# Adding B x u to one of the two states on TensorE, in PSUM, in 378 of 512 pairs of time steps

## Chip, cores and metric

One core of a Trainium2 chip. The metric is the device time of one execution of the kernel, in microseconds (us).

## What is computed

Two sequences of 1024 tokens with 512 channels go through a selective state-space layer (with a residual and a layer norm) and a gated feed-forward layer (with a residual and a layer norm), all in fp32. The core of it is the recurrence over time, with a state of 512 x 128 numbers for each sequence:

```python
def step(h, inp):
    dt, bt, ct, xt = inp
    h = jnp.exp(dt[:, :, None] * A) * h + (dt * xt)[:, :, None] * bt[:, None, :]
    y = jnp.einsum('bdn,bn->bd', h, ct)
    return (h, y)
...
x = _layernorm(x + (ys + x * D_param) @ out_proj_w.T)
x = _layernorm(x + (silu(x @ w_gate.T) * (x @ w_up.T)) @ w_down.T)
```

Here `dt`, `bt`, `ct` come from projections of a normalized and gated x, `u = dt * xt`, and B and C below are `bt` and `ct`.

## The kernel before

The state h has its index n (128) on the partitions and the 512 channels of a sequence in the free dimension. For each of the 1024 steps t and each of the two sequences b there are two VectorE instructions of 128 x 512: a product `a * h(t-1)` into PSUM (`m_ps`, line 708; one bank per sequence), and a sum into the ring `h` of seven steps (H_RING). The sum is a multiply-add `u * B + product` with B as a scalar for each partition (line 731), or, where another engine has multiplied u by B beforehand, a plain add (line 728). GpSimd does that for some even steps (line 615), ScalarE for others (line 1023).

The other engines supply and drain this loop:

- GpSimd spreads dt over diagonals (`dexp`, line 603), TensorE multiplies them by A (`exponents`, line 1223, four 32-row groups side by side) and ScalarE takes exp of the result into the ring `a` (line 1004). Each such round serves half the channels of four steps, so there is one for each pair of steps. The PSUM banks `p_ps` hold one round, so TensorE and ScalarE take turns on them.
- SP loads u of each step, broadcast to all partitions, from a scratch in DRAM into the ring `u_bc` of seven steps (line 472).
- TensorE computes y of a step from h and C (`y_row`, line 1299; 32-column matmuls, four side by side for two steps). It issues the y rows of steps t-2 and t-1 at each even t. ScalarE takes a window of 64 steps out at a time.
- Everything else (the projections for the chunk of 128 steps ahead, the output projection, layer norms and feed-forward for the chunk behind) is cut into pieces. `timetable` writes down in which half step ("slot") each piece stands, from gaps that are given by hand for each stage. All engines walk the same plan: two slots for each step, hence four for a pair. TensorE's pieces (`gu`, `down`, `sel`, `xp`, ...) share one PSUM bank, `work`, which ScalarE empties. A product piece (`product`, line 1059, or line 1199 for `down`) is four fp32 matmuls of 256 columns; the trace shows two records for each fp32 matmul.

All engines run their instructions strictly in the order in which they were written, with semaphores between them: `s_m` counts products, `s_h` sums, `s_y` y rows, `s_exp` the exponentials.

## Time and profile before

| | |
|---|---|
| median of 3 runs | 2670.15 us (2664.76 to 2670.43) |
| span of the profiled execution | 2662.4 us |
| VectorE busy | 2577.2 us, 97% of the span |
| TensorE busy (matmuls) | 2323.3 us, 87% |
| TensorE weight loads | 1281.6 us, 48% |
| ScalarE busy | 1836.4 us, 69% |
| GpSimd busy | 1030.8 us, 39% |

The span is the time from the first to the last instruction in one profiled execution; for that execution no other time is given. Busy times are unions of the records of an engine. In the names of the trace DVE is VectorE, ACT ScalarE, POOL GpSimd, PE TensorE's matmuls and PEld its weight loads.

### The profile page before, as it was taken

To read this page: it belongs to the slowest core of one execution; us is meant where nothing else is said; L and a number is where in the kernel's file an instruction comes from. 1 tells how busy PE (TensorE), PEld (TensorE's weight loads), DVE (VectorE), ACT (ScalarE), POOL (GpSimd) and SP (SyncE) were. 2 spreads that over 40 slices of the span, in tenths; PEclk is the share of its full clock that TensorE was granted. 3 is DMA by queue.
4 is the path that set the end of the run, shared out by engine and by line. 5 is a ranking of instruction groups with operands and counts; after the bars stand their busy time and mean duration, and the time that the engine had idled before them with its cause. 6 is when DMAs were issued, how large, how long until landed. Compare 5 with 4: busy or idle time off the path is not lost.

```text
span 2662.4 us, 48762 instructions
## 1 busy us (share of the span) xinstructions
PE 2323.3 (87%) x17036; PEld 1281.6 (48%) x17036; DVE 2577.2 (97%) x4160; ACT 1836.4 (69%) x2432; POOL 1030.8 (39%) x1031
## 2 busy tenths in 40 slices
PE   7867678999789987899889998899978998998898
PEld 4322234545345544555445553454534554465557
DVE  6999999999999999999999999999999999999892
ACT  5778767678676776667766777767867678653743
POOL 2343333443344433444334433344334443343320
PEclk8999999999899998999999999999989999999999
DMA  5666666777667776777767787677766777787784
GB/s 189 216 215 223 225 237 238 276 257 275 239 243 272 269 270 228 252 268 276 264 231 264 258 287 246 233 278 257 271 245 231 272 265 268 264 289 281 246 323 156
DMA packets 192064, 672.20 MB, mean 252 GB/s; under 512 B 20944, under 2 KB 26064, under 8 KB 191824
## 3 DMA queue, kind: packets, MB, share of 16 engines
q1 hardware_dynamic: 152432, 544.02, 57.8%
q10 hardware_dynamic: 39392, 125.06, 13.8%
q8 instruction: 140, 2.29, 0.3%
q14 instruction: 100, 0.82, 0.1%
HBM read 660.61 MB, written 8.39 MB: 251 GB/s over the span
## 4 chain that ended last, share of the span: by engine, by line
PE 45%; DVE 25%; ACT 14%; issue 11%; DMA 4%; DVEq 0%; ACTq 0%; POOL 0%; POOLq 0%
PE banks L1059 14%; PE banks L1223 11%; DVE h L731 11%; PE banks L1299 9%; DVE banks L708 9%; PE banks L1199 8%; ACT a L1004 6%; DVE h L728 5%; DMA U<-in_xT 2%; ACT L742 1%; ACT u_bc L1023 1%; DMA u_bc<-u_scratch 1%; PE banks L1151 1%; PE banks L1147 1%; DMA w_ring<-in_down_w 1%
## 5 line engine op out<-in xcount | busy, mean ns | idle before, releaser
L708 DVE TENSOR_TENSOR banks<-a,h 128x512 f32<-128x512 f32 x2048 | 1331.5, 692 | 6.9 <-ACT a L1004 6.9
L1004 ACT ACTIVATE a<-banks 128x2048 f32<-128x2048 f32 x512 | 960.3, 1876 | 510.1 <-PE banks L1223 464.8
L731 DVE SCALAR_TENSOR_TENSOR h<-u_bc,BCt,banks 128x512 f32<-128x512 f32 x1285 | 899.0, 734 | 5.9 <-PE banks L1299 5.8
L603 POOL TENSOR_TENSOR dexp<-spread,dt 128x512 f32<-128x512 f32 x512 | 538.5, 1052 | 815.2 <-DVE banks L708 765.7
L1299 PE MATMUL banks<-h,cz 128*32 128x512 f32 x4096 | 696.7, 618 | 97.6 <-DVE h L728 50.0
L1223 PE MATMUL banks<-dexp,A 32*128 32x256 f32 x8192 | 612.1, 414 | 149.6 <-ACT a L1004 147.8
L1223 PEld LDWEIGHTS banks<-dexp,A 32*128 32x128 f32 x8192 | 383.9, 191 | 474.7 <-ACT a L1004 354.5
L728 DVE TENSOR_TENSOR h<-u_bc,banks 128x512 f32<-128x512 f32 x763 | 489.8, 674 | 3.3 <-POOL u_bc L615 3.3
L1059 PE MATMUL banks<-vT,w_ring 128*128 128x256 f32 x1792 | 453.2, 396 | 18.7 <-ACT up L971 17.6
L1059 PEld LDWEIGHTS banks<-vT,w_ring 128*128 128x128 f32 x1792 | 326.0, 192 | 187.7 <-issue 108.8
L1023 ACT ACTIVATE u_bc<-u_bc,BCt 128x512 f32<-128x512 f32 x497 | 333.2, 713 | 61.7 <-DMA u_bc<-u_scratch 60.9
L615 POOL TENSOR_SCALAR u_bc<-u_bc,BCt 128x512 f32<-128x512 f32 x266 | 184.0, 692 | 379.7 <-DVE banks L708 379.7
L1299 PEld LDWEIGHTS banks<-h,cz 128*32 128x32 f32 x4096 | 109.0, 109 | 382.5 <-issue 370.0
L1199 PE MATMUL banks<-gated,w_ring 128*128 128x256 f32 x896 | 225.1, 394 | 16.0 <-ACT vT L976 8.9
L1199 PEld LDWEIGHTS banks<-gated,w_ring 128*128 128x128 f32 x896 | 162.1, 191 | 100.1 <-issue 65.4
L969 ACT ACTIVATE sg<-banks 128x256 f32<-128x256 f32 (+1 forms) x144 | 51.8, 360 | 143.4 <-PE banks L1059 141.9
L543 POOL TENSOR_TENSOR gated<-gated,sg 128x512 f32<-128x512 f32 x56 | 75.0, 1340 | 96.1 <-DVE banks L708 75.5
L546 POOL TENSOR_TENSOR gated<-gated,up 128x512 f32<-128x512 f32 x56 | 72.5, 1294 | 78.3 <-DVE banks L708 78.3
L742 ACT ACT_TABLE_LOAD x55 | 70.6, 1283 | 14.5 <-issue 12.3
L1059 PE MATMUL banks<-U,w_sel 128*128 128x256 f32 x256 | 70.5, 425 | 8.3 <-ACT dt L770 7.1
L973 ACT ACTIVATE sg<-sg,half 128x256 f32<-128x256 f32 (+1 forms) x144 | 71.4, 496 | 0.0
L1059 PEld LDWEIGHTS banks<-U,w_sel 128*128 128x128 f32 x256 | 51.2, 210 | 34.6 <-issue 15.7
(179 smaller groups left out, 1276.1 us busy)
## 6 DMA issues: line engine op xcount, KB each, us to landing
u_bc<-u_scratch SPq DMA_DIRECT2D x1021, 512.0 KB, 4.6
w_ring<-in_gu_w ACTq DMA_DIRECT2D x112, 512.0 KB, 5.0
w_ring<-in_down_w ACTq DMA_DIRECT2D x56, 512.0 KB, 5.3
a<-in_gu_w ACTq DMA_DIRECT2D x16, 512.0 KB, 5.6
a<-in_down_w ACTq DMA_DIRECT2D x8, 512.0 KB, 4.6
x_tok<-in_x_rows SPq DMA_DIRECT2D x15, 256.0 KB, 4.8
out_rows<-v ACTq DMA_DIRECT2D x15, 256.0 KB, 4.2
U<-in_xT ACTq DMA_DIRECT2D x7, 512.0 KB, 7.0
```

The source lines that it names most:

```text
L603: e.tensor_tensor(dexp[:, q % E_RING, :, :, :], spread[:, :].unsqueeze(1).unsqueeze(1).to_broadcast(shape), by_step[:, :, first:first + BS ...
L615: e.tensor_scalar(part, part, BCt[c % 2][:, 0, tl:tl + 1], 1.0, ALU.mult, ALU.mult).then_inc(s_zp, 1)
L708: e.tensor_tensor(m_ps[:, b, :], a[:, blk % A_RING, b, s, :], h[:, (t - 1) % H_RING, b * D:(b + 1) * D], ALU.mult).then_inc(s_m, 1)
L728: e.tensor_tensor(h[:, t % H_RING, part], u_bc[:, t % U_RING, part], m_ps[:, b, :], ALU.add).then_inc(s_h, 1)
L731: e.scalar_tensor_tensor(h[:, t % H_RING, part], u_bc[:, t % U_RING, part], BCt[c % 2][:, 0, b * TB + tl:b * TB + tl + 1], m_ps[:, b, :], ...
L742: e.preload_act_table_set("natural_log_exp_and_others")
L1004: e.activation(dst.rearrange("p b t (x j) -> p x (b t) j", j=GP), src.rearrange("p g (i r j) -> p (g i) r j", i=PAIR, j=GP), ACT.Exp, scal ...
L1023: e.activation(part, part, ACT.Copy, scale=BCt[c % 2][:, 0, b * TB + tl:b * TB + tl + 1]).then_inc(s_za, 1)
L1059: last = e.matmul(dst, w, x, start=i == 0, stop=i == len(pairs) - 1)
L1199: last = e.matmul(dst, tile[:, sub * (HB // 4) + i, :], hidden(x, hb), start=hb == 0, stop=hb == HB - 1)
L1223: last = e.matmul(dst[:, g, i * COLS:(i + 1) * COLS], A[rows, q % 2 * PAIR + i, :], lays, start=True, stop=True)
L1299: last = e.matmul(y_ps[group * GP:(group + 1) * GP, :], cz[:, first:first + GP], h[:, t % H_RING, b * D:(b + 1) * D], start=i == 0, stop=i ...
```

## The change

Steps are now walked in pairs (t, t+1), t even. From step 128 on, a pair is marked (`on_x`) where the summed load figures of ScalarE's pieces (`LOAD`) stay within a budget of 20 for each pair, with what exceeds it carried over to the next. 378 of 448 pairs are marked, 54 in each chunk. In a marked pair:

- VectorE leaves out the sum of (t, 1). TensorE adds it instead: a matmul with one row, B of the step as weights (1 x 128) and u as the moving operand (1 x 512), accumulates onto the product in PSUM (`add_inputs`).
- The product of (t+1, 1) reads h of (t, 1) there, in PSUM, and is written to `m_sb` in SBUF. It waits for the matmul (`s_acc`).
- ScalarE copies h of (t, 1) from PSUM to the ring `h` for y (`state`), after that product; the product of (t+2, 1), which overwrites the bank, waits for the copy (`s_hx`).
- The product of (t+1, 0) stands directly behind the sum of (t, 0).

For this, u comes in two rings (`u_bc` of seven steps for b = 0, `v_bc` of four for b = 1, which skips marked steps), and rows of u and B together (640 numbers) are written to a second DRAM scratch once for each chunk and loaded one by one into `x_row` by SP. B of sequence 1 is transposed for that by one more matmul per chunk. ScalarE's scaling of u is kept only in the first chunk and for b = 0, GpSimd's only for steps that are not marked. GpSimd's work in marked pairs waits for another product than before. In the last two chunks' feed-forward work the gap before `down` is 4 slots instead of 0.

```diff
+        on_x, busy = {}, 0
+        for t in range(FIRST_X, SEQ, 2):
+            busy = max(0, busy + sum(LOAD.get(stage, 0) for stage, _ in at_steps(t, 2)) - X_BUDGET)
+            if not busy:
+                on_x[t] = len(on_x)
...
+                e.dma_start(u_bc[:, slot, :], u_scratch[t, 0, :].partition_broadcast(P)).then_inc(d_u[slot], 16)
+                if t not in on_x:
...
+                    e.dma_start(v_bc[:, k % V1_RING, :], u_scratch[t, 1, :].partition_broadcast(P)
+                                ).then_inc(d_v[k % V1_RING], 16)
+                if t + X_AHEAD in on_x:
...
+                    e.dma_start(row_of(k), x_scratch[t + X_AHEAD:t + X_AHEAD + 1, :]).then_inc(d_row[k % X_RING], 16)
...
+            def product(t, b, dst):
+                blk, s = t // BS, t % BS
+                src = h[:, (t - 1) % H_RING, b * D:(b + 1) * D]
+                if b and t - 1 in on_x:
+                    e.wait_ge(s_acc, on_x[t - 1] + 1)
+                    src = m_ps[:, b, :]
+                elif t:
+                    e.wait_ge(s_h, sum_of(t - 1, b))
+                if b and t - 2 in on_x:
+                    e.wait_ge(s_hx, on_x[t - 2] + 1)
+                e.tensor_tensor(dst, a[:, blk % A_RING, b, s, :], src, ALU.mult).then_inc(s_m, 1)
...
+                product(t, 0, m_ps[:, 0, :])
+                product(t, 1, m_ps[:, 1, :])
...
+                total(t, 0, m_ps[:, 0, :])
+                if t in on_x:
+                    product(t + 1, 0, m_ps[:, 0, :])
+                    product(t + 1, 1, m_sb[:, :])
+                else:
+                    e.wait_ge(s_m, BATCH * t + 2)
+                    total(t, 1, m_ps[:, 1, :])
+                    product(t + 1, 0, m_ps[:, 0, :])
+                    product(t + 1, 1, m_ps[:, 1, :])
...
+            def state(t):
+
+                e.wait_ge(s_m, BATCH * (t + 2))
+                e.wait_ge(s_y, t - H_RING + 1)
+                e.activation(h[:, t % H_RING, D:], m_ps[:, 1, :], ACT.Copy).then_inc(s_hx, 1)
...
+                    if i and t - 1 in on_x:
+                        state(t - 1)
...
+            def add_inputs(t):
+
+                k = on_x[t]
+                row = row_of(k)
+                e.wait_ge(d_row[k % X_RING], 16 * (k // X_RING + 1))
+                e.wait_ge(s_m, BATCH * (t + 1))
+                e.matmul(m_ps[:, 1, :], row[:, D:], row[:, 0:D], start=False, stop=True, skip_group_check=True
+                         ).then_inc(s_acc, 1)
...
                     if i == 0 and t % 2 == 0 and t:
                         y_row(t - 2)
                         y_row(t - 1)
+                    if i and t in on_x:
+                        add_inputs(t)
```

On VectorE, in the middle of the recurrence, the order of two pairs before is this (`banks` is the product in PSUM):

```order
L708 TENSOR_TENSOR banks<-a,h 128x512 x2
L731 SCALAR_TENSOR_TENSOR h<-u_bc,BCt,banks 128x512 x2
L708 TENSOR_TENSOR banks<-a,h 128x512 x2
L731 SCALAR_TENSOR_TENSOR h<-u_bc,BCt,banks 128x512 x2
L708 TENSOR_TENSOR banks<-a,h 128x512 x2
```

and with the change, in marked pairs, this:

```order
L768 TENSOR_TENSOR banks<-a,h 128x512 x2
L790 SCALAR_TENSOR_TENSOR h<-u_bc,BCt,banks 128x512
L768 TENSOR_TENSOR banks<-a,h 128x512
L768 TENSOR_TENSOR m_sb<-a,banks 128x512
L790 SCALAR_TENSOR_TENSOR h<-u_bc,BCt,banks 128x512
L790 SCALAR_TENSOR_TENSOR h<-v_bc,BCt,m_sb 128x512
L768 TENSOR_TENSOR banks<-a,h 128x512 x2
```

Seven instructions stand where eight stood; the one that is gone is the second of the first two sums, and the two products of the second step have moved up, one of them right behind the sum it reads.

On TensorE, in a part of a chunk with feed-forward pieces (`banks<-vT,w_ring`), the order before is this:

```order
L1299 MATMUL banks<-h,cz 32x512 x4
L1059 MATMUL banks<-vT,w_ring 128x256 x4
L1223 MATMUL banks<-dexp,A 128x256 x8
L1299 MATMUL banks<-h,cz 32x512 x4
L1059 MATMUL banks<-vT,w_ring 128x256 x4
L1223 MATMUL banks<-dexp,A 128x256 x8
L1059 MATMUL banks<-vT,w_ring 128x256 x4
L1299 MATMUL banks<-h,cz 32x512 x4
```

and with the change this (L1409 are the y rows, L1322 the exponents, L1392 the addition):

```order
L1392 MATMUL banks<-x_row 128x512
L1322 MATMUL banks<-dexp,A 128x256 x8
L1156 MATMUL banks<-vT,w_ring 128x256 x4
L1409 MATMUL banks<-h,cz 32x512 x4
L1392 MATMUL banks<-x_row 128x512
L1156 MATMUL banks<-vT,w_ring 128x256 x4
L1322 MATMUL banks<-dexp,A 128x256 x8
L1409 MATMUL banks<-h,cz 32x512 x4
L1392 MATMUL banks<-x_row 128x512
L1156 MATMUL banks<-vT,w_ring 128x256 x4
L1322 MATMUL banks<-dexp,A 128x256 x8
L1156 MATMUL banks<-vT,w_ring 128x256 x4
```

The addition stands behind the y rows of the two steps before and behind what the plan has in the first slot of its pair, ahead of the exponents and the other pieces.

On ScalarE, in the part with the second feed-forward product, the order before is this:

```order
L1004 ACTIVATE a<-banks 128x8x8x32
L1023 ACTIVATE u_bc<-u_bc,BCt 128x512
L938 DMA w_ring<-in_down_w 128x1024
L1023 ACTIVATE u_bc<-u_bc,BCt 128x512 x2
L1004 ACTIVATE a<-banks 128x8x8x32
L1023 ACTIVATE u_bc<-u_bc,BCt 128x512 x3
```

and with the change this:

```order
L1094 ACTIVATE a<-banks 128x8x8x32
L1111 ACTIVATE h<-banks 128x512
L1094 ACTIVATE a<-banks 128x8x8x32
L1028 DMA w_ring<-in_down_w 128x1024
L1066 ACTIVATE vT<-banks 128x256
L1111 ACTIVATE h<-banks 128x512
```

The scalings of u are gone, and one copy of h stands in each marked pair, behind an exponential and, in places, a piece of the plan.

## Rows read from the trace of the kernel before

**Rows 1.** The page: busy time of each engine, share of the span, instructions.
```profile
PE 2323.3 (87%) x17036; PEld 1281.6 (48%) x17036; DVE 2577.2 (97%) x4160; ACT 1836.4 (69%) x2432; POOL 1030.8 (39%) x1031
```
**Rows 2.** One stretch by windows: length, PE, PEld, DVE, ACT, POOL busy, clock, DMA, GB/s.
```profile
760.00:1090.00 330.00, 294.13 (x2144) 162.28 (x2136) 330.00 (x531) 237.09 (x308) 134.97 (x133) 0.96 0.73 256
```
**Rows 3.** Groups by line and shape: busy us, mean ns | idle us before, released by.
```profile
L708 DVE TENSOR_TENSOR banks<-a,h 128x512 f32<-128x512 f32 x2048 | 1331.5, 692 | 6.9 <-ACT a L1004 6.9
...
L731 DVE SCALAR_TENSOR_TENSOR h<-u_bc,BCt,banks 128x512 f32<-128x512 f32 x1285 | 899.0, 734 | 5.9 <-PE banks L1299 5.8
...
L1223 PE MATMUL banks<-dexp,A 32*128 32x256 f32 x8192 | 612.1, 414 | 149.6 <-ACT a L1004 147.8
...
L728 DVE TENSOR_TENSOR h<-u_bc,banks 128x512 f32<-128x512 f32 x763 | 489.8, 674 | 3.3 <-POOL u_bc L615 3.3
L1059 PE MATMUL banks<-vT,w_ring 128*128 128x256 f32 x1792 | 453.2, 396 | 18.7 <-ACT up L971 17.6 <-DMA w_ring<-in_gu_w 0.2
```
**Rows 4.** VectorE's timeline in mid-recurrence: start us, length us, engine, line, instruction.
```profile
1007.14 1.29 DVE L708 TENSOR_TENSOR banks<-a,h 128x512 f32<-128x512 f32 x2
1008.34 0.68 DVE L728 TENSOR_TENSOR h<-u_bc,banks 128x512 f32<-128x512 f32 x1
1008.94 0.74 DVE L731 SCALAR_TENSOR_TENSOR h<-u_bc,BCt,banks 128x512 f32<-128x512 f32 x1
1009.60 1.29 DVE L708 TENSOR_TENSOR banks<-a,h 128x512 f32<-128x512 f32 x2
```
**Rows 5.** VectorE's timeline: the recurrence's first row, and the row behind it.
```profile
37.37 1.30 DVE L708 TENSOR_TENSOR banks<-a,h 128x512 f32<-128x512 f32 x2 [2.90 <-ACT a L1004]
...
2599.28 0.68 DVE L526 TENSOR_TENSOR v<-x_tok,d_skip 128x512 f32<-128x512 f32 x1
```
**Rows 6.** VectorE's timeline at the start: an instruction that reads its neighbour's result.
```profile
25.07 0.42 DVE L675 TENSOR_SCALAR t_both<-t_both 128x512 f32<-128x512 f32 x1
25.53 0.69 DVE L678 SCALAR_TENSOR_TENSOR t_both<-t_both 128x512 f32<-128x512 f32 x1
```
**Rows 7.** Timeline at the start: ScalarE copies that wait for matmuls, and matmuls for copies.
```profile
39.87 0.60 ACT L875 ACTIVATE u_bc<-banks 128x512 f32<-128x512 f32 x1 [0.26 <-PE banks L1284]
...
40.58 0.30 PEld L1284 LDWEIGHTS banks<-t_both,ident 128*128 128x128 f32 x2 [0.56 <-issue]
...
41.74 0.60 ACT L875 ACTIVATE u_bc<-banks 128x512 f32<-128x512 f32 x1 [0.26 <-PE banks L1284]
```
**Rows 8.** TensorE's timeline: matmuls with 512 columns, and the group behind them.
```profile
222.65 1.98 PE L1147 MATMUL banks<-w_out,ymod 128*128 128x512 f32 x4
...
224.47 1.02 PE L1148 MATMUL banks<-x_tok,ident 128*128 128x512 f32 x2
...
225.42 1.15 PE L1223 MATMUL banks<-dexp,A 32*128 32x256 f32 x16
```
**Rows 9.** TensorE's timeline: a group of exponents behind an idle stretch.
```profile
1001.98 2.09 PE L1223 MATMUL banks<-dexp,A 32*128 32x256 f32 x16 [2.50 <-ACT a L1004]
```
**Rows 10.** TensorE's timeline where one piece follows the other.
```profile
1215.78 1.99 PE L1059 MATMUL banks<-vT,w_ring 128*128 128x256 f32 x8
1217.70 1.06 PE L1299 MATMUL banks<-h,cz 128*32 128x512 f32 x8
1218.70 1.15 PE L1223 MATMUL banks<-dexp,A 32*128 32x256 f32 x16
1219.78 1.16 PE L1065 MATMUL banks<-ident,U 128*128 128x128 f32 x8
1220.86 1.06 PE L1299 MATMUL banks<-h,cz 128*32 128x512 f32 x8
```
**Rows 11.** ScalarE's timeline: first and last row of a feed-forward evacuation; a 128x512 copy.
```profile
1211.56 0.38 ACT L969 ACTIVATE sg<-banks 128x256 f32<-128x256 f32 x1
...
1212.37 0.52 ACT L973 ACTIVATE sg<-sg,half 128x256 f32<-128x256 f32 x1
...
1221.69 0.59 ACT L816 ACTIVATE t_both<-banks 128x512 f32<-128x512 f32 x1
```

More of the change, by code:

```diff
@@ L29 @@
 U_RING = 7
+V1_RING = 4
+FIRST_X = TB
+ROW = D + N
+X_RING = 4
+X_AHEAD = 0
+X_BUDGET = 20
 Z_AHEAD = 4
@@ L131, in stages_behind @@
             yield from [("gm*", hb // 2, 0), ("gp*", hb // 2, 0)]
-    yield "rest", 0, 2 * wide
+    yield "rest", 0, 2 if wide else GROUP
     for m in range(KB):
@@ L336, in build @@
         d_u = [sem(f"d_u{i}") for i in range(U_RING)]
+        d_v = [sem(f"d_v{i}") for i in range(V1_RING)]
+        d_row = [sem(f"d_row{i}") for i in range(X_RING)]
+        d_split = sem("d_split")
+        s_acc, s_hx = sem("s_acc"), sem("s_hx")
         d_w = [sem(f"d_w{i}") for i in range(W_RING)]
@@ L620, in gpsimd @@
                 c = t // TB
-                if t in DEXP_AT:
+                late = t in on_x and not has_piece(t + 1)
+                if t in DEXP_AT and not late:
                     e.wait_ge(s_m, BATCH * (t + 1))
                     diagonals(DEXP_AT[t])
+                if t - 1 in DEXP_AT and t - 1 in on_x and not has_piece(t):
+                    e.wait_ge(s_m, BATCH * t + 1)
+                    diagonals(DEXP_AT[t - 1])
                 if t % 2:
@@ L714, in vector @@
+            for t in range(0, SEQ, 2):
+                c, tl = t // TB, t % TB
+                if t % BS == 0:
+                    e.wait_ge(s_exp, 2 * (t // BS + 1))
+                product(t, 0, m_ps[:, 0, :])
+                product(t, 1, m_ps[:, 1, :])
                 if t == 0:
@@ L1091, in before @@
                     m = (1, 2, 0)[j]
-                    product(dst[:, 0:TC], [(w_xp[:, k, m * P:(m + 1) * P], U[:, k, :]) for k in range(KB)]
-                            ).then_inc(s_xp, 1)
+                    last = product(dst[:, 0:TC], [(w_xp[:, k, m * P:(m + 1) * P], U[:, k, :]) for k in range(KB)])
+                    if j == 1:
+                        last = e.matmul(dst[:, TC:TC + N], BCt[x % 2][:, 0, TB:], ident[:, :], start=True, stop=True)
+                    last.then_inc(s_xp, 1)
                 elif stage == "dtp":
@@ L1273, in first_chunk @@
                     for k in (2, 3):
-                        last = u_columns(ut_first(b), b, k)
+                        last = u_columns(ut_first(b), b, k, False)
                     last.then_inc(s_ut, 1)
```

131 lines of the change are left out of this document (79 added, 52 removed).

## The prediction

> **What bounds the kernel now.** I read the page first. VectorE is busy 97% of the span and TensorE 87% [rows 1], so there are two engines to think about. The windows view of a stretch with the feed-forward work in it shows VectorE busy for all of its 330 us, TensorE for 294.13 us, at a granted clock of 0.96 [rows 2]. By the grouped lines, VectorE's time is the recurrence and nothing else: 2048 products, 1285 multiply-adds, 763 plain adds, with under 17 us of waits before them in all [rows 3]. VectorE's own timeline gives the price of each by start-to-start distance, since neighbours overlap: two products take 1.20 us, a plain add 0.60, a multiply-add 0.66 [rows 4]. A pair of steps (4 products, 4 sums) of multiply-adds alone is 2.40 + 2.64 = 5.04 us. The recurrence starts at 37.37 and its last sum ends where the next VectorE row begins, at 2599.28 [rows 5]: 2561.9 us for 512 pairs, 5.00 each. 63.1 us of other work follow. So VectorE bounds the kernel, and a removed sum is worth 0.66 us only if nothing else then takes the time.
>
> **What VectorE gains.** In 378 pairs one multiply-add goes. But product (t+1, 0) now stands directly behind the sum (t, 0) that it reads. Where a VectorE instruction waits for its neighbour it starts 0.04 us after that one's end (25.07 + 0.42 to 25.53) [rows 6]; the sum lasts 0.73 us, so it costs 0.77 instead of 0.66. A pair is then 0.60 x 4 for the products, 0.77 and two times 0.66: 4.49 us. The plain adds fall from 763 to 82 by the built program; I price all ordinary pairs at 5.04. VectorE alone would thus give 378 x 4.49 + 134 x 5.04 = 2373 us, 189 us under the 2562 of now.
>
> **What the new chain costs.** Product (t+1, 1) waits for TensorE, and TensorE for product (t, 1). The round trip is not in the loop of before, but the start of the kernel has its shape, one fp32 matmul with 512 columns between two ScalarE copies: the copy from 39.87 ends at 40.47, the weight load starts at 40.58 and the next copy at 40.88 belongs to the other stream; the one that this matmul releases starts at 41.74 [rows 7]. That is 0.11 us in and 1.16 us through. Lower bound of the trip: 1.02 us, the two passes of such a matmul alone [rows 8]; upper bound 2.1 us, if TensorE runs at half clock, where a group that takes 1.15 us takes 2.09 [rows 9]. I take 1.16, the row with the same shape. Counting from the start a of the addition on TensorE: product (t+1, 1) at a + 1.16, the two sums, then the two products of the next pair, so product (t+2, 1) starts at a + 1.16 + 0.60 + 0.66 + 0.66 + 0.60 = a + 3.68, ends 0.69 later, and the next addition can start at **a + 4.48**. If TensorE is always free, nothing is lost.
>
> **It is not free.** TensorE's stretch at full clock shows pieces that follow each other with no gap, so their start-to-start distance is what TensorE needs, whatever its busy share means: exponents 1.08 us, a feed-forward or projection piece (4 fp32 matmuls, 256 columns) 1.92, the y rows of two steps 1.00, a group of four transposes 1.08 [rows 10]. The addition is two passes with 512 columns: 0.95 us to the next group [rows 8]. For its cost from both sides: at least the 0.86 us of two starts 0.43 apart, at most 1.9 at half clock; one row instead of 128 does not shorten it, as 32-row matmuls of 256 columns last 414 ns, full ones 396 [rows 3]. TensorE's order in a pair of the changed program is y rows of t-2 and t-1, then what the plan puts into the first of the four slots (w0), the addition, exponents, then the pieces of the other three slots (w). From one addition to the next, a' - a is the largest of three:
> - VectorE's chain: 4.48.
> - The chain over y: h of (t+1, 1) is done at a + 1.16 + 0.60 + 0.66 + 0.73 = 3.15, the y row starts 0.11 later and is taken at the same 1.00, then w0: 4.26 + w0.
> - TensorE's own sum: 0.95 + 1.08 + w + 1.00 + w0 = 3.03 + w + w0.
>
> Each pair pays its own maximum. The addition is a meeting of both engines, so TensorE can't save up slack in light pairs for heavy ones, as it does now through the ring of seven h. I counted the 378 pairs in the plans of the program (projection out: 1.82 and 2.77, the former from [rows 8]; the last chunk's half-wide pieces half as long):
> - 78 light ones, or followed by an ordinary pair: 4.6 us, 358 us.
> - 155 with one piece behind the addition (3.03 + 1.92 = 4.95): 767 us.
> - 22 with about 1.1 us of work ahead of it: 5.25, 116 us.
> - 47 with a piece of 1.92 ahead of it: 6.18, 290 us.
> - 76 with two pieces or more (3.03 + 3.84 = 6.87 and up): 528 us.
>
> Sum 2059 us, 5.45 a pair against 5.00 now. The plan favours this: the pairs left out are those heavy for ScalarE, and they hold little TensorE work.
>
> **Other edits.** Chunk 0 has no addition: 320 us as now. The other 70 ordinary pairs: 5.10 each, 357 us (0.06 for TensorE entering them late; 0 to 0.5). ScalarE loses nearly all its scalings of u and gets 378 copies of about 0.59 us [rows 11]. Its copy of h has from the end of product (t+1, 1) at a + 1.85 to a + 3.68, so 1.83 us for 0.11 + 0.59; nothing is added for it, except below. VectorE's operands in SBUF instead of PSUM: 0, since a product with both inputs in SBUF costs 0.60 like an add with one in PSUM [rows 4]. SP issues one row of 2.5 KB more and half of the broadcast less in these pairs; it runs seven steps (17 us) ahead, so 0. GpSimd is busy 39% and only starts elsewhere: 0. The extra transpose per chunk: 7 x 0.3 = 2 us, within the 357. Half clock: 0.96 granted means some 8% of time at the lower of 1.2 and 2.4 GHz; after an idle wait of 2.50 us the exponents ran at it [rows 9]. The addition fills such waits; gain and loss bounded by 8% of 378 pairs times 5 us, 150 us, and taken as 0.
>
> **Sum.** 37.4 + 320 + 2059 + 357 + 63.1 = 2836.5 us of span against 2662.4 now. No other time stands with the profiled execution than its span; the median of the runs is 2670.15, 7.8 more, which I carry over: **2844 us**, 174 slower (6.5%).
>
> **Rivals.**
> - *TensorE does not limit (0.12).* Pieces overlap with the waiting after all and every pair takes 4.48: 37.4 + 320 + 1693 + 353 + 63.1 + 7.8 = 2474 us, faster. For it: weight loads cover only 48% of the span [rows 1]. Against: rows 10 show no gap in which a 0.95 us group would fit.
> - By "Trainium Kernel Development and Optimization", section Performance Expectations, of the Trainium skill, matmul busy time is a bad metric, since matmuls are pipelined, and the share of weight loads a good one; by that rule this rival is the likely case, 2474 us. The trace has 87% for the one and 48% for the other, and in rows 10 TensorE is full all the same.
> - *TensorE limits, but is never kept waiting (0.12).* Then only its sum counts: per chunk 129 us of pieces, 64 x 2.08 for exponents and y rows, 54 x 0.95: 313.5 us against 320 now; 348 in the last chunk, 37.4 + 320 + 6 x 313.5 + 348 + 63.1 + 7.8 = 2657 us, faster by 0.5%. Against: the 47 pairs in which y stands in the chain.
> - *ScalarE's copy comes late (0.13).* In 68 of the pairs a feed-forward evacuation, 1.33 us from 1211.56 to 1212.37 + 0.52 [rows 11], stands ahead of the copy in ScalarE's queue, in 79 others something shorter. It decides once such a piece ends over 1.1 us after product (t+1, 1). At 1.33 and 0.6 us each that is up to 138 us: 2980.
>
> **Numbers.** The forecast itself, 2750 to 2910, gets 0.60; 0.03 is left for other things. A difference under 0.2%, 5.3 us, can't be told from none. Faster: 0.25 (both rivals and a hundredth over); same: 0.03; slower: 0.72. The range leaves out the full gain and the tail of the last rival: 2640 to 2960.
>
> **What would show it.** Right: VectorE's idle time grows from 17 us to some 350, most of it ahead of the product that reads PSUM, and released by the addition; additions of 592 ns a pass; pairs of 4.5, 5, 6.2 and 6.9 us in the order of the plan; TensorE's busy time near 2650 us. Wrong: product rows that start 0.60 apart nearly everywhere (then it is the first rival), or VectorE waiting for ScalarE's copy more than for the addition (the last one). The weakest step is that a pair pays its own maximum.

## The result, and the profile after

The changed kernel takes **2962.11 us**, median of 4 runs (2960.09 to 2965.39), beside 2668.95 for the one before: 1.11 times as long, interval 1.1082 to 1.1118. I had said 2844, at most 2960. So the sign was right, and the loss is 293 us where 174 were forecast. The profiled execution has a span of 2963.6 us at a granted clock of 0.975.

The page of the changed kernel gives busy time, share of the span and instructions, as in [rows 1]:

```profile
PE 2682.3 (91%) x17806; PEld 1465.5 (49%) x17806; DVE 2477.1 (84%) x3782; ACT 1721.8 (58%) x2329; POOL 889.8 (30%) x838
```

VectorE went from 97% to 84%: it lost 378 instructions and got idle time. TensorE went from 87% to 91%. A stretch with feed-forward work, by windows as in [rows 2], and the chain of work that ended last, by engine (before, the chain lay 45% on PE and 25% on DVE):

```profile
740.00:1120.00 380.00, 352.92 (x2328) 189.20 (x2324) 323.81 (x489) 235.17 (x315) 117.57 (x107) 0.99 0.59 189
```

```profile
PE 63%; DVE 13%; ACT 12%; issue 11%; DMA 1%; DVEq 0%; ACTq 0%
```

The groups by line and shape, as in [rows 3]: busy us, mean ns | idle us before, released by:

```profile
L768 DVE TENSOR_TENSOR banks<-a,h 128x512 f32<-128x512 f32 x1670 | 1156.4, 727 | 19.2 <-ACT a L1094 4.1 <-ACT h L1111 2.2
...
L790 DVE SCALAR_TENSOR_TENSOR h<-u_bc,BCt,banks 128x512 f32<-128x512 f32 x942 | 697.7, 741 | 0.7 <-PE banks L1409 0.7
...
L1392 PE MATMUL banks<-x_row 1*128 1x512 f32 x756 | 424.0, 640 | 7.1 <-DVE banks L768 7.1
...
L790 DVE SCALAR_TENSOR_TENSOR h<-v_bc,BCt,m_sb 128x512 f32<-128x512 f32 x378 | 283.3, 749 | 0.0
L768 DVE TENSOR_TENSOR m_sb<-a,banks 128x512 f32<-128x512 f32 x378 | 259.5, 686 | 391.1 <-PE banks L1392 389.9
L1111 ACT ACTIVATE h<-banks 128x512 f32<-128x512 f32 x378 | 225.8, 597 | 791.1 <-DVE m_sb L768 784.6
```

The waits (engine, line, waited for: us, times, longest) show who holds whom:

```profile
ACT h L1111 <- DVE m_sb L768: 784.6, 342, 6.2
...
DVE m_sb L768 <- PE banks L1392: 389.9, 264, 10.2
...
PEld banks L1322 <- ACT a L1094: 198.7, 142, 5.5
...
PE banks L1322 <- ACT a L1094: 79.3, 67, 4.0
```

VectorE waits 389.9 us for additions, all of it ahead of the product that reads the addition's result (`m_sb`); for ScalarE's copy it waits 2.2 us in all. In 333 of the marked pairs the pair before is marked too. In the trace, the 333 distances from the addition before to theirs sum to 1883 us; by the prediction's classes they are 4.5 us for light pairs (4.48 forecast), 5.04 on average with one piece behind the addition (4.95; most are 4.8, a few up to 8.0), 6.22 with a piece ahead of it (6.18), 6.89 with two pieces (6.87). A pair whose chain goes over y looks like this (TensorE's rows in the changed kernel):

```profile
908.48 0.69 PE L1392 MATMUL banks<-x_row 1*128 1x512 f32 x1
...
911.10 1.75 PE L1409 MATMUL banks<-h,cz 128*32 128x512 f32 x8 [0.63 <-DVE h L790]
912.78 1.13 PE L1198 MATMUL banks<-rstd,w_dt 128*128 128x256 f32 x4
913.84 0.69 PE L1392 MATMUL banks<-x_row 1*128 1x512 f32 x1
```

TensorE waits 0.63 us for the last h, writes the y rows, does the piece that the plan put first, and adds 5.36 us after the last addition.

What the 333 distances don't hold is how such a run of marked pairs **begins**. There are 45 first additions, each behind an ordinary pair. The product that such an addition reads is done 1.4 us after the start of the pair's first product. TensorE starts the 45 additions 95 us later than that in all, 2.1 us each: 13 are not late, 7 are late by 0.9 us, 11 by 1.75, and 14 by 3.1 to 11.2. TensorE's timeline at one of the 14 (4.55 us late), then ScalarE's and VectorE's:

```profile
921.14 1.99 PE L1156 MATMUL banks<-vT,w_ring 128*128 128x256 f32 x8
923.06 1.06 PE L1409 MATMUL banks<-h,cz 128*32 128x512 f32 x8
925.87 1.15 PE L1322 MATMUL banks<-dexp,A 32*128 32x256 f32 x16 [1.75 <-ACT a L1094]
928.12 1.99 PE L1156 MATMUL banks<-vT,w_ring 128*128 128x256 f32 x8 [1.10 <-ACT up L1061]
930.05 1.06 PE L1409 MATMUL banks<-h,cz 128*32 128x512 f32 x8
931.04 1.99 PE L1156 MATMUL banks<-vT,w_ring 128*128 128x256 f32 x8
932.97 0.69 PE L1392 MATMUL banks<-x_row 1*128 1x512 f32 x1
```

```profile
918.83 1.28 ACT L825 ACT_TABLE_LOAD   x1
...
923.96 1.86 ACT L1094 ACTIVATE a<-banks 128x2048 f32<-128x2048 f32 x1
925.84 1.28 ACT L1059 ACT_TABLE_LOAD   x1
```

```profile
928.99 1.00 DVE L768 TENSOR_TENSOR banks<-a,h 128x512 f32<-128x512 f32 x1
934.12 0.69 DVE L768 TENSOR_TENSOR m_sb<-a,banks 128x512 f32<-128x512 f32 x1 [4.14 <-PE banks L1392]
```

In the two ordinary pairs before, ScalarE runs a softplus (six instructions of 0.6 to 0.7 us between two loads of its function table) and empties the exponents' PSUM late. TensorE waits 1.75 and 1.10 us for it, still does a piece that stands ahead of the addition (931.04), and VectorE stands for 4.14 us.

### The profile page after: what moved, and what is told of

Read it like the earlier page. It is cut to its first block, busy times and chain, and to the rows that moved or that the text cites. A ratio compares the mean times of both kernels' runs of the same rounds, so it can differ in the third digit from the quotient of the medians.

```text
span 2963.6 us, 51957 instructions
## 1 busy us (share of the span) xinstructions
PE 2682.3 (91%) x17806; PEld 1465.5 (49%) x17806; DVE 2477.1 (84%) x3782; ACT 1721.8 (58%) x2329; POOL 889.8 (30%) x838
## 4 chain that ended last, share of the span: by engine, by line
PE 63%; DVE 13%; ACT 12%; issue 11%; DMA 1%; DVEq 0%; ACTq 0%
PE banks L1156 18%; PE banks L1409 12%; PE banks L1322 11%; PE banks L1392 9%; PE banks L1298 8%; DVE h L790 8%; ACT a L1094 4%; DVE banks L768 3%; ACT L825 2%; DVE h L788 1%; PE banks L1250 1%; DVE m_sb L768 1%; PE banks L1246 1%; ACT L1059 1%; PE banks L1222 0%
## 5 line engine op out<-in xcount | busy, mean ns | idle before, releaser
L768 DVE TENSOR_TENSOR banks<-a,h 128x512 f32<-128x512 f32 x1670 | 1156.4, 727 | 19.2 <-ACT a L1094 4.1
L1322 PE MATMUL banks<-dexp,A 32*128 32x256 f32 x8192 | 791.1, 413 | 80.0 <-ACT a L1094 79.3
L1409 PE MATMUL banks<-h,cz 128*32 128x512 f32 x4096 | 710.9, 617 | 149.1 <-DVE h L790 138.2
L790 DVE SCALAR_TENSOR_TENSOR h<-u_bc,BCt,banks 128x512 f32<-128x512 f32 x942 | 697.7, 741 | 0.7 <-PE banks L1409 0.7
L1111 ACT ACTIVATE h<-banks 128x512 f32<-128x512 f32 x378 | 225.8, 597 | 791.1 <-DVE m_sb L768 784.6
L1322 PEld LDWEIGHTS banks<-dexp,A 32*128 32x128 f32 x8192 | 504.9, 189 | 341.6 <-ACT a L1094 198.7
L768 DVE TENSOR_TENSOR m_sb<-a,banks 128x512 f32<-128x512 f32 x378 | 259.5, 686 | 391.1 <-PE banks L1392 389.9
L1392 PE MATMUL banks<-x_row 1*128 1x512 f32 x756 | 424.0, 640 | 7.1 <-DVE banks L768 7.1
L1409 PEld LDWEIGHTS banks<-h,cz 128*32 128x32 f32 x4096 | 117.5, 109 | 443.8 <-issue 426.6
L790 DVE SCALAR_TENSOR_TENSOR h<-v_bc,BCt,m_sb 128x512 f32<-128x512 f32 x378 | 283.3, 749 | 0.0
L1392 PEld LDWEIGHTS banks<-x_row 1*128 1x128 f32 x756 | 110.9, 183 | 244.3 <-issue 240.2
L790 DVE SCALAR_TENSOR_TENSOR h<-v_bc,BCt,banks 128x512 f32<-128x512 f32 x268 | 198.0, 739 | 0.0
L667 POOL TENSOR_SCALAR u_bc<-u_bc,BCt 128x512 f32<-128x512 f32 x73 | 50.5, 692 | 105.7 <-DVE banks L768 75.8
```

The source lines that it names most:

```text
L768: e.tensor_tensor(dst, a[:, blk % A_RING, b, s, :], src, ALU.mult).then_inc(s_m, 1)
L790: e.scalar_tensor_tensor(h[:, t % H_RING, part], u, BCt[c % 2][:, 0, b * TB + tl:b * TB + tl + 1], src, ALU.mult, ALU.add).then_inc(s_h, 1)
L1111: e.activation(h[:, t % H_RING, D:], m_ps[:, 1, :], ACT.Copy).then_inc(s_hx, 1)
L1322: last = e.matmul(dst[:, g, i * COLS:(i + 1) * COLS], A[rows, q % 2 * PAIR + i, :], lays, start=True, stop=True)
L1392: e.matmul(m_ps[:, 1, :], row[:, D:], row[:, 0:D], start=False, stop=True, skip_group_check=True).then_inc(s_acc, 1)
L1409: last = e.matmul(y_ps[group * GP:(group + 1) * GP, :], cz[:, first:first + GP], h[:, t % H_RING, b * D:(b + 1) * D], start=i == 0, stop=i ...
```

## Experiments

Where an expectation numbers its theories, 1 is the prediction's (each marked pair pays its own maximum where the two engines meet), 2 is TensorE's load alone, 3 is a price for the trip to TensorE and back in every marked pair, whatever stands around it, 4 is GpSimd working beside VectorE. "Before" was run again beside each (2665.97 to 2671.43 us).

### Load without a meeting

To the kernel before, one fp32 matmul of 512 columns is added in 364 pairs. Nobody waits for it and nothing uses its sum (the matrix it multiplies is zero).

```diff
+            def extra(t):
...
+                if mid:
+                    e.matmul(y_ps[3 * GP:4 * GP, :], zeros[:, :], d_skip[:, :], start=False, stop=False)
...
+                    if i and t in marked:
+                        extra(t)
```

> The kernel before, with one fp32 matmul of 512 columns more (zero weights, so nothing is added to y) at the place of the addition in 364 of the 378 marked pairs, for which nobody waits. TensorE gets about the load of the change, without the meeting. Theory 1 (the meeting): TensorE's sum is 312 us of 320 in a chunk and the ring of seven h evens out heavy and light pairs, so 2665 to 2700. Theory 2 (load alone): 2900 or more, as in the changed kernel.

2844.39 us, ratio 1.0642 (1.0626 to 1.0658): +173 us, between the theories.

```profile
PE 2557.4 (90%) x17764; PEld 1324.9 (47%) x17764; DVE 2700.9 (95%) x4161; ACT 1836.4 (65%) x2432; POOL 1092.7 (38%) x1031
```

So the load alone costs 173 us with no one waiting for the result. A ring of seven h doesn't hide it. TensorE ends at 90% busy as the changed kernel does at 91%. Of the 282 us that are left it waits 136.9 us for ScalarE, which has the exponents' PSUM. VectorE's products also last 752 ns here, 692 in the kernel before, 119 us in all.

The same with half the columns:

```diff
-                    e.matmul(y_ps[3 * GP:4 * GP, :], zeros[:, :], d_skip[:, :], start=False, stop=False)
+                    e.matmul(y_ps[3 * GP:4 * GP, 0:D // 2], zeros[:, :], d_skip[:, 0:D // 2], start=False, stop=False)
```

> The kernel before with the extra matmul that nobody awaits cut from 512 to 256 columns in the 364 pairs (its sum is used by nothing). With 512 columns it was 2844.39 us, 173 us over the kernel before. If TensorE's load costs in proportion: near 2757 us. If it costs nothing until TensorE is nearly full and then all of its length: 2680 to 2720 us.

2739.3 us, 1.027 (1.0246 to 1.0293): +72 us by the ratio. That is 42% of the price for half of the work: 0.20 us a pair for the first 256 columns, 0.27 for the next. This is nearer to proportional (2757) than to free room below a threshold (2680 to 2720).

Is it GpSimd? In the version with 512 columns GpSimd's gate products stand beside VectorE's, and both get longer. They are cut to 8 columns (the gate is then not applied to the rest):

```diff
-                e.tensor_tensor(pair, pair, sg[:, ring, 0:columns_of(x)], ALU.mult).then_inc(s_gm, 1)
+                few = slice(0, 8)
+                e.tensor_tensor(pair[:, :, few], pair[:, :, few], sg[:, ring, few], ALU.mult).then_inc(s_gm, 1)
...
-                e.tensor_tensor(pair, pair, up[:, ring, 0:columns_of(x)], ALU.mult).then_inc(s_gated, 1)
+                few = slice(0, 8)
+                e.tensor_tensor(pair[:, :, few], pair[:, :, few], up[:, ring, few], ALU.mult).then_inc(s_gated, 1)
```

> The kernel before with the extra matmuls that nobody waits for (2844 us), and GpSimd's two multiplications of the feed-forward's gates cut from 256 or 128 columns to 8; the rest of these products is left out. In that run VectorE's products lasted 752 instead of 692 ns in the mean, while GpSimd waited 297 us for ScalarE's gates and then ran several instructions in a row. Theory 4 (the late GpSimd instructions run beside VectorE's products and stretch them): 2670 to 2740. Theory 2 (TensorE's load alone is the bound): 2820 to 2844, since TensorE's work is the same.

2849.67 us, 1.0654 (1.0605 to 1.0702): no gain, although VectorE's busy time fell by 62 us, to 2639.2; its waits took them up. Its products still last 720 ns, so 55 us of the lengthening stay in this version. And the changed kernel with GpSimd's diagonals at a quarter of their size (the exponents are then incomplete):

```diff
-                shape = [P, PAIR * BATCH, BS, GP]
+                n = BS if q < 4 * E_RING else 1
+                shape = [P, PAIR * BATCH, n, GP]
...
```

> The changed kernel, with GpSimd's diagonals written for one of four steps only (three quarters of each instruction are left out, old values stay). In the changed kernel 183 products of VectorE last 1.00 instead of 0.69 us, each beside such an instruction that starts behind the second product of a pair. Theory 4 (GpSimd beside the product costs): the 183 shrink to 0.69 and the time falls by up to 57 us, 2905 to 2940. Theory 1 with TensorE late in most of these pairs: less than 10 us of it comes through, 2952 to 2966.

2964.94 us, 1.1112 (1.1092 to 1.1132), as theory 1 had it. Its groups:

```profile
L769 DVE TENSOR_TENSOR banks<-a,h 128x512 f32<-128x512 f32 x1670 | 1099.5, 692 | 20.2 <-ACT a L1095 4.1 <-ACT h L1112 3.2
...
L769 DVE TENSOR_TENSOR m_sb<-a,banks 128x512 f32<-128x512 f32 x378 | 259.4, 686 | 443.5 <-PE banks L1393 443.5
```

The products fell from 727 to 692 ns, 57 us in all, and the wait for the addition grew from 389.9 to 443.5 us: what VectorE gains it hands to the wait. In the marked pairs TensorE sets the pace.

### The size of the addition, and of the work around it

In the changed kernel, the addition on 128 of its 512 columns (the other sums lack B x u):

```diff
-                e.matmul(m_ps[:, 1, :], row[:, D:], row[:, 0:D], start=False, stop=True, skip_group_check=True
+                e.matmul(m_ps[:, 1, 0:P], row[:, D:], row[:, 0:P], start=False, stop=True, skip_group_check=True
```

> The changed kernel, with the addition cut to 128 of its 512 columns; the input of the other three quarters of sequence 1 is left out in the marked steps. TensorE's cost of an addition falls from 0.95 to some 0.3 us, the trip from 1.16 to 0.5. Theory 2 (TensorE's load, wherever it is): 378 x 0.65 = 250 us less, near 2715. Theory 1 (the meeting behind other pieces): only pairs that wait gain; by the chains of the prediction 165 us less, near 2795. If the meeting cost nothing at all beyond the load, it would be below 2669.

2787.01 us, 1.0442 (1.0424 to 1.0461), 8 us from theory 1's figure and 72 from theory 2's. By the trace the 333 distances fall from 1883 to 1718 us, the 165 us that theory 1 gave; the 45 first additions are still 92 us late. Next, the feed-forward products cut to one matmul of four, in the kernel before as a control and in the changed one (both leave those products incomplete):

```diff
-                    last = product(dst[:, g * TC:g * TC + cols], [(gu[:, g, k, :], vT(x)[:, k, :]) for k in range(KB)])
+                    last = product(dst[:, g * TC:g * TC + cols], [(gu[:, g, k, :], vT(x)[:, k, :]) for k in range(1)])
...
+                        if i == 0:
...
```

> The control for the run before: the kernel before, with the same three quarters of the feed-forward products left out. VectorE bounds it by all theories, so 2669 within 0.5%. If it is faster by more, TensorE was already part of the bound before the change.

2625.84 us, 0.9824 (0.9809 to 0.9839), more than the 0.5% that I allowed. The two profiled executions are 38 us apart: 18.7 us of it lie between the first product and the last (2560.0 to 2541.3 us by the trace, 12 us of them in the last chunk), the rest behind it. TensorE's work was thus a small part of what bounds the recurrence before the change, mostly in its last chunk.

> The changed kernel, with one of four matmuls in each gate, up and down piece of the feed-forward layer; the other three quarters of those products are left out. Pieces of 1.92 us become some 0.6 us, nothing else moves. Theory 1 (TensorE's pieces hold the addition up): 260 to 350 us less, 2610 to 2700. Theory 3 (round trip): over 2900. If VectorE's chain of 4.48 us a pair then rules nearly everywhere, the time is near 2550.

2716.94 us, 1.0166 (1.015 to 1.0181): 91 us above its control, outside the 2610 to 2700 expected. VectorE still waits 176.1 us for the addition. So with the feed-forward work cut to a quarter the meeting still costs: the 45 first additions are 75 us late in all, and y rows and smaller pieces still stand ahead of additions. Less load helps by 245 us, and doesn't make the edit pay.

### The addition at the head of the pair

```diff
+                    if i == 0 and t in on_x:
+                        add_inputs(t)
                     if i == 0 and t % 2 == 0 and t:
                         y_row(t - 2)
                         y_row(t - 1)
-                    if i and t in on_x:
-                        add_inputs(t)
```

The addition now stands ahead of the y rows and of the plan's piece in the first slot.

> The changed kernel, with TensorE issuing the addition at the head of its pair, ahead of the y rows of the two steps before and of the plan's piece in the first slot. Theory 1 (the meeting: VectorE waits in a pair for whatever stands ahead of the addition in TensorE's queue): the waits behind y rows and first-slot pieces go, TensorE's own sum stays; by the same sums of rows that gave 2844 us this saves about 105 us, so 2962 becomes 2840 to 2880. Theory 2 (load alone: TensorE simply has too much work, wherever the addition stands): 2962, unchanged within 0.5%. Theory 3 (the round trip of VectorE to TensorE and back costs in every pair): unchanged as well.

2986.81 us, 1.1169 (1.1151 to 1.1188): 25 us slower instead of some 100 faster. In its groups:

```profile
L768 DVE TENSOR_TENSOR banks<-a,h 128x512 f32<-128x512 f32 x1670 | 1160.5, 726 | 93.9 <-ACT h L1111 77.8 <-ACT a L1094 3.2
...
L1392 PE MATMUL banks<-x_row 1*128 1x512 f32 x756 | 422.5, 639 | 56.0 <-DVE banks L768 55.8
```

VectorE now waits 77.8 us for ScalarE's copy, which comes late behind the exponents, and still 332.0 for the addition. TensorE now stands still for 55.8 us ahead of the addition until product (t, 1) is there (7.1 us in the changed kernel), with the y rows behind it. The third rival, ScalarE's late copy, is real in this order alone. The granted clock is 0.944, 0.975 in the changed kernel; its share of the 25 us was not separated.

The run shows one thing besides, at the first additions. In the changed kernel 18 of the 45 are late by 0.9 or 1.75 us, all with a piece ahead of them in their own pair; with the addition ahead of that piece all 18 start within 0.04 us of where they could. Over all 45 the lateness falls from 95 to 56 us; the 333 distances grow by 54.

### Additions in the lightest pairs alone

Additions only where the plan puts no TensorE work ahead of them and at most one piece behind the last one: 47 pairs in place of 378, with the scaling of u on ScalarE restored for the first sequence.

```diff
-            if not busy:
+            if not busy and not products_near(t):
```

> The changed kernel with 47 marked pairs instead of 378: only those with no TensorE piece ahead of the addition and at most one transpose-sized piece behind the last one; ScalarE's scaling of u is back for sequence 0 in unmarked pairs, and GpSimd's (412 plain adds). By theory 1 each of these pairs takes 4.5 us as VectorE's chain alone: 47 x 0.55 = 26 us gained against the kernel before, 351 plain adds fewer at 0.06 = 21 us lost: 2655 to 2670. If the meeting costs in every pair, over 2680.

2729.3 us, 1.0243 (1.0223 to 1.0263), so 2655 to 2670 was missed. VectorE waits only 47.3 us for additions; the wait that grew is another (before: 60.9 us, 72 times):

```profile
ACT u_bc L1138 <- DMA u_bc<-u_scratch: 358.5, 157, 7.7
```

u is late: SyncE's queue stands at the ring of four v, and u's loads stand behind v's. With the first chunk's 41 pairs as well (`FIRST_X = 16`, 88 in all):

> The same with additions also in the first chunk, from step 16 on, where TensorE has no feed-forward work: 88 marked pairs, 350 plain adds. By theory 1: 88 x 0.55 = 48 us gained, 413 plain adds fewer = 25 us lost, so 2640 to 2655, faster than both kernels. By theory 3 (a cost in each marked pair) it is slower than the run with 47.

2735.49 us, 1.026 (1.0235 to 1.0285), with the same wait (301.7 us), and missed as well. Both again, with u issued three steps ahead of v:

```diff
+            for t in range(FIRST_U, FIRST_U + U_AHEAD):
+                load_u(t)
             for t in range(FIRST_U, SEQ):
+                if t + U_AHEAD < SEQ:
+                    load_u(t + U_AHEAD)
```

> As the version with 47 marked pairs, but SyncE issues the loads of u three steps ahead of those of v instead of behind them. If the late u was what cost there (ScalarE waited 358.5 us for u from DMA, against 60.9 before): that wait comes back near 60 us and the time to 2650 to 2670 us. If instead each meeting in PSUM costs wherever it is put: the DMA wait falls all the same and the time stays near 2729 us.

> As the version with 88 marked pairs (those of the first chunk among them), with u loaded three steps ahead of v. If the late u was the cost and TensorE has room in the first chunk: 2640 to 2655 us, faster than both kernels. If a meeting costs wherever it is put: near 2735 us.

2704.3 us, 1.0143 (1.0116 to 1.0171), and 2699.34 us, 1.0122 (1.0105 to 1.014). The wait for u:

```profile
ACT u_bc L1146 <- DMA u_bc<-u_scratch: 78.1, 71, 4.2
```

So the late u cost 25 and 36 us; the 2650 to 2670 and 2640 to 2655 were missed. To part what is left, the same rings and the same rule for scalings with no additions at all, and with those of the first chunk alone:

```diff
-        for t in range(FIRST_X, SEQ, 2):
+        for t in range(FIRST_X, LAST_X, 2):
```

(`LAST_X` is 16 for none, `TB` for the first chunk.)

> As the version with u loaded three steps ahead and its two rings and 763 - 350 fewer scalings, but with no marked pair at all. If the 47 meetings cost nothing where TensorE has room and the rings and lost scalings cost the 38 us: 2700 us, as with them. If the meetings cost: 2666 plus some 25 us for the scalings that are missing (0.06 us each, 413), so near 2690 us or below.

> As that, with marked pairs in the first chunk alone (41 of them), where TensorE is busy some 75%. In the version with 88 the first chunk took 309.5 us, with 47 it took 318.1. If a meeting gains where TensorE has room: 6 to 10 us below the version with no marks, and a first chunk near 309 us. If a meeting gains nowhere: at or above it.

2679.12 us, 1.0046 (1.0032 to 1.006), and 2670.68 us, 1.0007 (0.9999 to 1.0016). VectorE's timeline, first products of chunks 0 and 1, without additions and then with those of chunk 0:

```profile
37.53 1.30 DVE L798 TENSOR_TENSOR banks<-a,h 128x512 f32<-128x512 f32 x2 [3.15 <-ACT a L1124]
...
355.65 1.31 DVE L798 TENSOR_TENSOR banks<-a,h 128x512 f32<-128x512 f32 x2
```

```profile
38.35 1.30 DVE L798 TENSOR_TENSOR banks<-a,h 128x512 f32<-128x512 f32 x2 [3.18 <-ACT a L1124]
...
348.39 1.29 DVE L798 TENSOR_TENSOR banks<-a,h 128x512 f32<-128x512 f32 x2
```

318.1 against 310.0 us, as expected: in the chunk that has the least work beside the recurrence, an addition **gains** 0.20 us (8.1 us for 41). In the other chunks 47 additions, in the lightest pairs there are, cost 25 us (2704.3 - 2679.1), 0.54 each. The split of the ring and the fewer scalings cost 10 us by themselves. The best version thus can't be told from the kernel before; none beats it.

What VectorE waits for the sum, for the 47 additions (the version with 2704.3 us) and then for the 41 of the first chunk:

```profile
L795 DVE TENSOR_TENSOR m_sb<-a,banks 128x512 f32<-128x512 f32 x47 | 31.9, 680 | 33.1 <-PE banks L1419 33.1
```

```profile
L798 DVE TENSOR_TENSOR m_sb<-a,banks 128x512 f32<-128x512 f32 x41 | 27.9, 681 | 4.3 <-PE banks L1424 4.3
```

The 47 stand nearly alone: 39 of them follow an ordinary pair. 27 of the 39 are not late at all, and 12 are late by 33 us in all, up to 3.99. Ahead of that one TensorE waits 1.00 us for ScalarE, then does the exponents, a group of transposes and the y rows, and the product that it needs has long been there. So these additions lose by the same thing as the 45 of the changed kernel: TensorE is behind VectorE when the two have to meet. That these 33 us are the 25 of the time is argued from their size; no run took them away.

### What makes the first additions late

If TensorE's own work in the ordinary pairs does it, a cut there must help. 52 first feed-forward pieces in ordinary pairs (12 of them of half width, in the last chunk) lose three of four matmuls; for comparison, 49 pieces that stand alone behind an addition lose as much.

```diff
+        short = {(x, j) for c in range(1, CHUNKS) for slot in plans[c] for stage, x, j in plans[c][slot]
+                 if stage == "gu" and TB * c + slot // SLOTS // 2 * 2 not in on_x}
...
-                    last = product(dst[:, g * TC:g * TC + cols], [(gu[:, g, k, :], vT(x)[:, k, :]) for k in range(KB)])
+                    last = product(dst[:, g * TC:g * TC + cols], [(gu[:, g, k, :], vT(x)[:, k, :])
+                                                                   for k in range(1 if (x, j) in short else KB)])
```

> The changed kernel with the 52 first feed-forward pieces that stand in ordinary pairs cut from four matmuls to one (what they compute is left incomplete): 75 us of TensorE work less, at 1.44 each. If the 45 late entries carry the missing time: 50 to 75 us less than 2962, 2887 to 2912 us. If they don't, as the prediction had it with 0.06 us an ordinary pair: at most 10 less, 2950 to 2962 us.

> The changed kernel with the 49 feed-forward pieces that stand alone behind an addition, in marked pairs followed by a marked pair with nothing ahead of its addition, cut from four matmuls to one (what they compute is left incomplete): 71 us of TensorE work less. If each pair pays its own maximum (5.04 measured, 4.48 then): 27 us less, 2935 us. If only TensorE's total counts: 71 us less, 2891 us.

2969.81 us, 1.1127 (1.1112 to 1.1143), and 2941.96 us, 1.1025 (1.1007 to 1.1043). The second lies by "pays its own maximum" (20 us off, 27 said, 71 for the total). The first gives nothing, outside both figures: TensorE's work in the ordinary pairs isn't it. (With 12 pieces of half width the cut is 66 us of work, not 75. The pieces ahead of the first additions stand in marked pairs and were not cut.) The 45 first additions are 102 us late in this run, 95 in the changed kernel. The place shown above, in that run:

```profile
925.42 1.18 PE L1325 MATMUL banks<-dexp,A 32*128 32x256 f32 x16 [2.63 <-ACT a L1096]
927.67 1.22 PE L1158 MATMUL banks<-vT,w_ring 128*128 128x256 f32 x2 [1.07 <-ACT up L1063]
928.82 1.94 PE L1412 MATMUL banks<-h,cz 128*32 128x512 f32 x8
930.69 3.23 PE L1158 MATMUL banks<-vT,w_ring 128*128 128x256 f32 x8
933.85 0.69 PE L1395 MATMUL banks<-x_row 1*128 1x512 f32 x1
```

Here the wait for ScalarE is 2.63 us instead of 1.75 and the piece ahead of the addition takes 3.23 instead of 1.99 (the last section comes back to it); the addition starts later than without the cut. So ScalarE's pieces in the ordinary pairs were cut: softplus and layer norm lose their logarithm, with it the table loads, and most instructions run on 8 columns, one on GpSimd among them (neither is then computed); once alone, once with the cut of before.

```diff
-                    log_table()
+                    few = slice(0, 8)
...
-                    e.activation(t_exp, pre[:, :, :], ACT.Abs).then_inc(s_soft, 1)
+                    e.activation(t_exp[:, :, few], pre[:, :, few], ACT.Abs).then_inc(s_soft, 1)
...
-                    e.activation(T[:, both, :], t_exp, ACT.Ln, bias=one[:, :]).then_inc(s_soft, 1)
+                    e.activation(T[:, both, :], t_exp, ACT.Identity, bias=one[:, :]).then_inc(s_soft, 1)
```

> The changed kernel with ScalarE's softplus and layer norm pieces made short: no logarithm and so no load of its table in them (1.28 us each time, and back), and most of their other instructions on 8 columns; softplus and layer norm are thus not computed. That is some 4 us less of ScalarE in each such pair, and these pairs are ordinary ones. If ScalarE holds TensorE there, and so makes the next addition late: the waits of 2.85, 1.79 and 0.75 us ahead of the three late additions of a chunk go, 38 to 50 us in all, 2912 to 2924 us. If ScalarE isn't the cause: within 8 us of 2962.

> The same, and the first feed-forward pieces of ordinary pairs cut from four matmuls to one as before (which alone took nothing off). If the two engines cover each other there: the cut now counts, another 20 to 40 us, 2875 to 2900 us. If TensorE's work in ordinary pairs never matters: as the version with the short ScalarE pieces.

2905.81 us, 1.0881 (1.0842 to 1.0921), and 2905.76 us, 1.0876 (1.0842 to 1.091). The first took off 56 us, more than the 38 to 50 expected; the second nothing more, so the two engines don't cover for each other: with both cuts TensorE waits at this place for the last h (1.13 us) ahead of the y rows, and only the piece behind them makes the addition late. The same place with ScalarE's pieces cut:

```profile
912.16 1.15 PE L1324 MATMUL banks<-dexp,A 32*128 32x256 f32 x16
913.24 1.99 PE L1158 MATMUL banks<-vT,w_ring 128*128 128x256 f32 x8
915.16 1.24 PE L1411 MATMUL banks<-h,cz 128*32 128x512 f32 x8
916.33 1.99 PE L1158 MATMUL banks<-vT,w_ring 128*128 128x256 f32 x8
918.25 0.69 PE L1394 MATMUL banks<-x_row 1*128 1x512 f32 x1
```

No wait for ScalarE; the addition is 1.74 us late instead of 4.55. Over all 45, the lateness fell from 95.2 to 51.0 us, and the 333 distances from 1883.1 to 1869.3: 58 us together, the 56 that the time shows. What is left of the 51 us is nearly all behind the pieces ahead of first additions in their own pairs: 23 with one of 1.92 us are 44 us late, 7 with one of 1.09 are 6.

## Why the prediction was too low

By its own sum, against the profiled execution (2836.5 forecast, 2963.6 measured; the 7.8 us from span to time were 1.8 in this execution):

| Term | Forecast | Measured |
|---|---|---|
| before the recurrence | 37.4 | 40.6 |
| chunk 0 | 320 | 320.7 |
| chunks 1 to 7 | 2416 | 2535.6 |
| behind it | 63.1 | 66.7 |

Chunk 0 came out right by luck. The 320 us "as now" are an eighth of the recurrence of the kernel before; its chunk 0 took 314.1 us by the trace. The change takes 112 of its 160 plain adds away, where ScalarE no longer scales u, at 0.06 us 6.7 us more: the sum had neither. The term before the recurrence is 37 to 41 us in the profiled executions of all versions, so its 3 us say nothing.

- **The maximum of three chains held.** 333 distances sum to 1883 us where the classes give 1848. That a pair pays its own maximum, the weakest step by the prediction, was borne out, by the distances and by the cut in marked pairs. It was 35 us too low: by 0.09 in each of 150 pairs with one piece, 13 us, and by 9 us in 6 pairs with pieces of the output projection ahead of the addition and behind it, which take 8.3 us and stood with those of two pieces at 6.87. The rest is spread over the other classes.
- **The round trip of 1.16 us** from [rows 7] was the median of all 378, from the addition's start to the product that reads it.
- **The step that failed** is "78 light ones, or followed by an ordinary pair: 4.6 us" with "0.06 for TensorE entering them late". Both treat the border between ordinary and marked pairs as nearly free; about 9 us in all. The 45 entries measure 95: 86 of the 120 us missing in chunks 1 to 7. There are two causes, each about 45 us. First, my second bound, 4.26 + w0, holds for a first addition too: 23 of the 45 have a piece of 1.92 ahead of it (1.70 over the 4.48) and 7 have 1.09 (0.87), 45 us. I applied it inside the runs only. Two runs bear it out: with the addition ahead of the piece 18 of these 30 are no longer late, and with ScalarE's pieces short 51 us are left. Second, ScalarE: the pairs left out of the change were those heavy for it, and there it empties the exponents' PSUM late and holds TensorE just before the two must meet; 44 us go with its pieces. I had looked in these pairs for TensorE work, found little, and priced them at nothing.
- **Rivals.** TensorE does not limit: wrong, 173 us for load alone. The Trainium skill, "Trainium Kernel Development and Optimization", section Performance Expectations, says of the matmul share that it is a bad metric for the distance to roofline, and of the weight-load share that it is a good one. Read as a measure of free room, as the prediction read it, it would have misled: weight loads stayed at 47 to 49% while 364 more matmuls, at a matmul share of 87 to 90%, cost 6%. Only its sum counts: wrong, since a cut of 71 us in marked pairs gave 20. ScalarE's copy late: wrong, 2.2 us of waits, unless the addition is moved to the head.
- **Priced at nothing.** GpSimd's work beside VectorE does lengthen the products, by 57 us, and costs nothing all the same, by the version with small diagonals. The ring of four v shows no wait of VectorE for a load of u in the changed kernel, where ScalarE scales next to no u, and cost 25 to 36 us where it does. TensorE's clock: 0.99 granted in the stretch shown, 0.96 in the one before the change; no run separated its share.
- **Signs to look for**: VectorE idle 391 + 19 us ahead of its products (350 said), TensorE busy 2682 (2650 said), distances of 4.5, 5.0, 6.2 and 6.9, and 640 ns a pass of the addition in the mean, 587 at the least (592 said).

What stays open: how the 173 us of plain load split between TensorE's own sum and its waits with ScalarE, why TensorE is behind VectorE at 12 of the 47 lightest additions and not at the others, and what the first additions would cost with both of their causes taken away at once.

## What to carry to other kernels

Here an engine at 87% with a queue of mixed work had no 13% to give: 0.95 us of extra work in a pair cost half of that even where nobody waited for it. Where two engines hand a value back and forth in each step, the items ahead of it in either queue can turn into time, and so can the items of a third engine that one of them waits for. Price the first such step behind a free stretch with the same formula as those inside, and look there for an engine that has fallen behind. Moving an instruction off the busiest engine is worth trying only where the receiving one has room in that very stretch: here a gain of 0.20 us each in the first chunk, and a loss of 0.54 each over the others together.

## What the runs showed of the hardware

A VectorE product with both inputs in SBUF gets longer beside a GpSimd instruction. In the changed kernel 183 of 2048 products take 1.00 us instead of 0.69, each beside a GpSimd instruction that writes the diagonals; of the 378 products that read h in PSUM 219 have GpSimd beside them too, and none takes over 0.7 us. With the diagonals at a quarter of their size none of the 183 is left:

```profile
722.76 1.05 POOL L655 TENSOR_TENSOR dexp<-spread,dt 128x512 f32<-128x512 f32 x1 [3.93 <-DVE banks L768]
...
723.37 1.00 DVE L768 TENSOR_TENSOR banks<-a,h 128x512 f32<-128x512 f32 x1
```

In the version with 512 extra columns two products, 1.29 us otherwise, took 3.13 beside two GpSimd instructions, and the second of those took 1.72 instead of 1.27:

```profile
826.92 3.13 DVE L717 TENSOR_TENSOR banks<-a,h 128x512 f32<-128x512 f32 x2
827.78 1.72 POOL L554 TENSOR_TENSOR gated<-gated,up 128x512 f32<-128x512 f32 x1
```

TensorE was granted a lower clock in one stretch with waits. With its pieces in ordinary pairs cut, the granted clock of the place shown was 0.61, part of the time at the lower level of 1.2 GHz (1.00 in the changed kernel, from 925 to 933 us), and the piece ahead of the addition took 3.23 us instead of 1.99; windows of that run:

```profile
925.00:933.80 8.80, 7.31 (x34) 3.77 (x34) 4.49 (x7) 4.75 (x7) 3.59 (x3) 0.61 0.66 230
```

That the lower level comes from the waits of 2.63 and 1.07 us ahead of it is argued from the order of the rows, as in [rows 9]; no run separated it. It can be a part only of why the cut gave nothing back: with ScalarE's pieces short the granted clock of the whole run is 0.985, TensorE waits for no ScalarE at this place, and the same cut gives nothing either.
